# Cross attention on one core: seven late value units, the first loads in single chunks, and the low halves of x ahead of the maxima

## What is computed

```python
# x (32, 512, 640), ctx (32, 77, 1024), 20 heads of 32
q = heads(x @ to_q_w)
k, v = heads(ctx @ to_k_w), heads(ctx @ to_v_w)
p = softmax(einsum('bhqd,bhkd->bhqk', q, k) / sqrt(32))
out = merge(einsum('bhqk,bhkd->bhqd', p, v)) @ to_out_w + to_out_b + x
```

## Time and profile before

| | us |
|---|---|
| time, median of 3 runs | 1733.48 (1733.34 to 1733.49) |
| time of the profiled execution | 1733.08 |
| its span, first to last instruction | 1730.5 |
| TensorE busy | 1706.0 |
| VectorE busy | 1250.5 |
| ScalarE busy | 1082.2 |
| GpSimd busy | 599.3 |

### The profile page before, as it was taken

How to read it: one execution, slowest core, us unless ns; L and a number is a source line. 1 busy time by engine, 2 the same in 40 slices (tenths; PEclk the granted TensorE clock), 3 DMA queues, 4 the chain that set the end, 5 groups by cost and what they waited for, 6 DMA issues and landing times.

```text
span 1730.5 us, 38867 instructions
## 1 busy us (share of the span) xinstructions
PE 1706.0 (99%) x13551; PEld 1365.5 (79%) x13551; DVE 1250.5 (72%) x2525; ACT 1082.2 (63%) x5676; POOL 599.3 (35%) x814
## 2 busy tenths in 40 slices
PE   7999999999999999999999999999999999999998
PEld 7999999767777777777777777777777777777776
DVE  5222123778888888888888888888888888888874
ACT  4322123766767676776767676777767676776762
POOL 0211112433434343343434343333434343333341
PEclk9999999989999999999999999999999999999999
DMA  9544213878989889888979897979797989897965
GB/s 222 169 108 112 68 46 88 217 200 222 239 225 233 237 221 239 223 237 222 238 216 240 218 243 217 246 209 246 211 245 213 245 210 250 211 247 214 244 184 118
DMA packets 311920, 354.43 MB, mean 205 GB/s; under 512 B 40456, under 2 KB 196294, under 8 KB 311726
## 3 DMA queue, kind: packets, MB, share of 16 engines
q1 hardware_dynamic: 241422, 298.38, 64.8%
q10 hardware_dynamic: 66016, 40.97, 10.5%
q0 software_dynamic: 4288, 12.62, 2.1%
HBM read 173.07 MB, written 178.81 MB: 203 GB/s over the span
## 4 chain that ended last, share of the span: by engine, by line
PE 96%; ACT 2%; DVE 0%; DMA 0%; SPq 0%; issue 0%; ACTq 0%
PE p_ring L1099 32%; PE p_ring L1013 31%; PE p_scores L1022 9%; PE p_ring L1056 8%; PE p_bank L439 8%; PE p_bank L458 7%; ACT probs L779 2%; PE p_ring L458 1%; DMA x_raw<-in_L_xattn_to_k_w 0%; PE p_ring L1108 0%; SPq L262 0%; DVE neg_first L847 0%; PE p_scores L1072 0%; ACT x_t L808 0%; ACT o_t L798 0%
## 5 line engine op out<-in xcount | busy, mean ns | idle before, releaser
L742 POOL TENSOR_TENSOR probs<-probs,rsum 128x308 f32<-128x308 f32 x640 | 447.8, 702 | 436.0 <-DVE rsum L862 432.7
L1013 PE MATMUL p_ring<-x_t,wq_split 128*128 128x512 f32 x2400 | 581.5, 394 | 0.0
L1099 PE MATMUL p_ring<-o_t,wo_split 128*128 128x512 f32 x2385 | 568.4, 390 | 0.0
L1013 PEld LDWEIGHTS p_ring<-x_t,wq_split 128*128 128x128 f32 x2400 | 445.2, 188 | 146.9 <-ACT kv_out L790 52.8
L1099 PEld LDWEIGHTS p_ring<-o_t,wo_split 128*128 128x128 f32 x2385 | 446.2, 188 | 107.1 <-ACT kv_out L790 14.3
L779 ACT ACTIVATE probs<-p_scores,neg_first 128x77 f32<-128x77 f32 x1280 | 393.9, 363 | 18.8 <-DVE neg_second L850 18.8
L779 ACT ACTIVATE probs<-p_scores,neg_second 128x77 f32<-128x77 f32 x1280 | 401.5, 444 | 0.0
L779 ACT ACTIVATION_READ_ACCUMULATOR probs<-p_scores,neg_second 128x1 f32 x1280 | 374.9, 326 | 0.0
L870 DVE STREAM_TRANSPOSE turned<-probs 128x384 f32<-128x384 f32 x640 | 353.4, 554 | 26.5 <-POOL probs L742 26.2
L779 ACT ACTIVATION_READ_ACCUMULATOR probs<-p_scores,neg_first 128x1 f32 x1280 | 313.4, 245 | 0.0
L790 ACT ACTIVATE kv_out<-p_ring 128x512 f32<-128x512 f32 x79 | 47.2, 597 | 388.3 <-PE p_ring L1056 388.3
(11 more groups left out here) (48 smaller groups left out, 1186.8 us busy)
## 6 DMA issues: line engine op xcount, KB each, us to landing
p_scratch<-turned SPq DMA_DIRECT2D x158, 768.0 KB, 5.7
probs_t<-p_scratch SPq DMA_DIRECT2D x316, 256.0 KB
x_raw<-in_x ACTq DMA_DIRECT2D x124, 320.0 KB, 7.5
out<-out_blocks SPq DMA_DIRECT2D x124, 320.0 KB, 6.2
probs_t<-p_scratch SPq DMA_DIRECT2D x158, 104.0 KB
ctx_raw<-in_ctx SPq DMA_DIRECT2D x28, 256.0 KB, 7.3
k_sb<-k_scratch SPq DMA_DIRECT2D x32, 192.5 KB, 6.3
v_sb<-v_scratch SPq DMA_DIRECT2D x158, 38.5 KB
```

What stands on the lines that cost most here:

```text
L742: nc.gpsimd.tensor_tensor(heads_of(t), heads_of(t), rsum[:, n % 2, t, :].unsqueeze(2).to_broadcast([P, HG, N_TXT]), ALU.mult).then_inc(pro ...
L1013: last = nc.tensor.matmul(bank_of("Q", n)[:, :], wq_s[:, w, c, g * P:(g + 1) * P], x_t[:, a, c, :], start=c == 0 and i == 0, stop=c == CC ...
L1099: last = nc.tensor.matmul(bank_of("O", n)[:, :], wo_s[:, w, c, k * P:(k + 1) * P], o_t[b % 2][:, o, c, :], start=c == 0 and i == 0, stop=c ...
```

## The change

**Late units.** `LATE_UNITS` gets (8, 1) in front, so there are seven, F0 to F6; each of F0 to F5 now stands for the unit before the one it was. F6 (32 rows, as F5) is a 24-matmul unit in phase 3, between the scores and V. ScalarE's phase 3 is now `S0 S1 F6 K U V S2 ...` instead of `K U V S0 ...`: two tiles of exponentials first. GpSimd's is `F6 W N0 ...`. The last two units share slot 2 of `kv_out` (`out_slot`), since the value copies K use the first two slots; counts of stores per slot follow (`stored_before`), and SyncE waits for F0 to F2 before it issues the first reads of probs. In VECTOR_FIRST the turns Y10 and Y11 go from the end of phase 2 into phase 3, and Q3 of phase 3 goes behind Y13.

**Low halves of x.** For k mod 5 = 4, and so in phase 4 too, VECTOR has `Y14 L12 L13 L14 M W H` where it had `Y14 L13 M L14 W H` with L12 at the end of the phase before. SCALAR has `X14 K U V` where it had `K X14 U V`.

**First loads.** wk's first pair of chunks is loaded as two single chunks; the halves of ctx blocks 0 and 1 are loaded one at a time between wk's pairs, the third pair of chunks between the second half of block 0 and that of block 1. ScalarE, VectorE and TensorE work on the first two blocks in the same way, block 0's slices, the weights, then block 1's, and TensorE runs four units of block 0 for two slices and then four of block 1.

```diff
-                "K X14 U V S0 S1 S2 S3 S4 S5 S6 S7 D3")
+                "X14 K U V S0 S1 S2 S3 S4 S5 S6 S7 D3")
...
-TENSOR_FIRST = orders("S Q2 Q3 F1 F2", "S Q2 F3 F4 Q3", "S V Q2 Q3 F5", "S V Q2 Q3")
+TENSOR_FIRST = orders("S Q2 Q3 F1 F2", "S Q2 F3 F4 Q3", "S V Q2 Q3 F5", "S F6 V Q2 Q3")
...
-    LOADS = ([(wk, k, 2) for k in range(0, KC, 2)] + [(wv, k, 2) for k in range(0, KC, 2)]
+    LOADS = ([(wk, 0, 1), (wk, 1, 1)] + [(wk, k, 2) for k in range(2, KC, 2)] + [(wv, k, 2) for k in range(0, KC, 2)]
...
-    LATE_UNITS = [(BLOCKS - 2, u) for u in (2, 3)] + [(BLOCKS - 1, u) for u in range(VU)]
+    LATE_UNITS = [(BLOCKS - 2, u) for u in (1, 2, 3)] + [(BLOCKS - 1, u) for u in range(VU)]
...
+    def out_slot(n):
+
+        return n % OUTS if n < LATE + 5 else OUTS - 1
+
+    def stored_before(slot, n):
+
+        return DMA * len([i for i in range(n) if out_slot(i) == slot])
+
...
+        def load_first_half(j, half):
+            n0, c0 = j * TB // SQ, half * CK // 2
+            for i in range(I):
+                sp.dma_start(ctx_raw[i * SQ:(i + 1) * SQ, j, :, c0:c0 + CK // 2],
+                             ctx_v[i][:, n0:n0 + TB // SQ, c0:c0 + CK // 2]).then_inc(first_loaded[j][half], DMA)
+
+        load_first_half(0, 0)
         load_weights(range(0, 2))
-        load_first_halves(1)
-        load_weights(range(2, 4))
-        load_weights(range(4, 8))
+        load_first_half(1, 0)
+        load_weights(range(2, 3))
+        load_first_half(0, 1)
+        load_weights(range(3, 4))
+        load_first_half(1, 1)
+        load_weights(range(4, 5))
+        load_weights(range(5, 9))
...
         for u in range(TU):
-            for j in range(2):
-                context_high(j, u)
+            context_high(0, u)
             split_weights(WK[2 * u:2 * u + 2])
+            context_high(1, u)
...
         for u in range(TU):
-            for j in range(2):
-                turn_context(j, u)
-            for j in range(2):
-                context_low(j, u)
+            turn_context(0, u)
+            context_low(0, u)
             split_weights(WK[2 * u:2 * u + 2])
+            turn_context(1, u)
+            context_low(1, u)
...
-        for k in range(KC):
-            pe.wait_ge(w_split, k + 1)
-            for j, m in FIRST[:BANKS]:
-                keys_part(j, m, k)
+        for u in range(TU):
+            for block in range(2):
+                for k in (2 * u, 2 * u + 1):
+                    pe.wait_ge(w_split, k + 1)
+                    for j, m in FIRST[:BANKS]:
+                        if j == block:
+                            keys_part(j, m, k)
...
+                        if k == 1:
+                            sp.wait_ge(project["unit_done"], LATE + 3)
...
-                    project["wait_stored"](act, project["units"] - 1)
+                    project["wait_stored"](act, project["units"] - 2)
```

More of the change, by code:

```diff
@@ L228, in wait_stored @@
         for i in range(OUTS):
-            eng.wait_ge(unit_stored[i], DMA * len(range(i, n, OUTS)))
+            eng.wait_ge(unit_stored[i], stored_before(i, n))
     def sync(sp):
@@ L255, in load_weights @@
                           .then_inc(w_loaded[load], DMA)
-        def load_first_halves(half):
-            c0 = half * CK // 2
-            for j in range(2):
-                n0 = j * TB // SQ
-                for i in range(I):
-                    sp.dma_start(ctx_raw[i * SQ:(i + 1) * SQ, j, :, c0:c0 + CK // 2],
-                                 ctx_v[i][:, n0:n0 + TB // SQ, c0:c0 + CK // 2]).then_inc(first_loaded[j][half], DMA)
-        load_first_halves(0)
-        load_weights(range(0, 2))
-        load_first_halves(1)
-        load_weights(range(2, 4))
-        load_weights(range(4, 8))
+        def load_first_half(j, half):
[4 more added lines that the diff above has]
+        load_first_half(0, 0)
+        load_weights(range(0, 2))
+        load_first_half(1, 0)
[5 more added lines that the diff above has]
+        load_weights(range(5, 9))
         load_block(2)
-        load_weights(range(8, 11))
+        load_weights(range(9, 12))
         load_block(3)
-        load_weights(range(11, 14))
+        load_weights(range(12, 15))
         load_block(4)
@@ L285, in store_key @@
             pool.dma_start(k_scratch[m * P:(m + 1) * P, bass.ds(j * TB, tokens)],
-                           kv_out[:, n % OUTS, 0:tokens]).then_inc(unit_stored[n % OUTS], DMA)
+                           kv_out[:, out_slot(n), 0:tokens]).then_inc(unit_stored[out_slot(n)], DMA)
         def store_value(j, u):
@@ L292, in store_value @@
             pool.dma_start(v_scratch[bass.ds(j * TB + t0, rows), hf * HALF:(hf + 1) * HALF],
-                           kv_out[0:rows, n % OUTS, :]).then_inc(unit_stored[n % OUTS], DMA)
+                           kv_out[0:rows, out_slot(n), :]).then_inc(unit_stored[out_slot(n)], DMA)
         def store_values(j):
@@ L329, in keys_out @@
             if n >= OUTS:
-                act.wait_ge(unit_stored[n % OUTS], DMA * (n // OUTS))
-            nc.scalar.activation(kv_out[:, n % OUTS, 0:tokens], bank_of(n)[:, 0:tokens],
+                act.wait_ge(unit_stored[out_slot(n)], stored_before(out_slot(n), n))
+            nc.scalar.activation(kv_out[:, out_slot(n), 0:tokens], bank_of(n)[:, 0:tokens],
                                  ACT.Copy, scale=SCALE).then_inc(unit_copied, 1)
@@ L337, in value_out @@
             act.wait_ge(unit_done, n + 1)
-            act.wait_ge(unit_stored[n % OUTS], DMA * (n // OUTS))
-            nc.scalar.activation(kv_out[0:rows, n % OUTS, :], source[0:rows, 0:HALF],
+            act.wait_ge(unit_stored[out_slot(n)], stored_before(out_slot(n), n))
+            nc.scalar.activation(kv_out[0:rows, out_slot(n), :], source[0:rows, 0:HALF],
                                  ACT.Copy).then_inc(unit_copied, 1)
```

2 lines of the change are left out of this document (1 added, 1 removed), and 10 rows, old and new, of tables (SCALAR_FIRST, VECTOR, VECTOR_FIRST).

## The result

| | before | changed |
|---|---|---|
| time, median of 13 executions each (us) | 1733.18 (1731.94 to 1734.03) | 1736.43 (1734.07 to 1740.23) |
| ratio to before | | 1.0022, 95% interval 1.0015 to 1.0030 |
| profiled execution: time, span | 1733.08, 1730.5 | 1735.22, 1733.4 |

The forecast was 1734.2 us in a range of 1725 to 1739. The change costs 3.3 us where it was to cost 0.7, and its times spread over 6.2 us where those of before spread over 2.1 (in later sets of 17 executions those of before spread over 2.4 to 4.4 us). Nearly all the profile is as foretold.

What follows compares the result with a forecast made beforehand. The prediction took TensorE's waits and slow stretches to bound the kernel. Start -1.7, seventh late unit -3.8 and low halves +6.2 made +0.7, from 1733.48 to 1734.2 us, range 1725 to 1739.

Steps and rivals of the forecast that it cites:

- What bounds the kernel: Whole kernel: TensorE is busy 1706.0 of 1730.5 us, so a change pays only where TensorE stands or is slow.
- The start: First loads: TensorE starts at 8.65 instead of 12.59, values at 41.1 instead of 42.84; 1.7 us gained.
- what is late next: At the start, the ninth unit waits for the first unit's copy behind a ScalarE weight split, starting at about 35.4.
- that load is limited by bytes that the change does not alter: At the start, wv's chunks 4 and 5 still end loading at 33.35; four extra issues could cost 0.2 us.
- The seventh late unit: Phases 3 and 4: next scores at 16.4, phase 4 ends at 36.7, against 40.5 in all before; 3.8 us gained.
- with no drop of the clock: Phases 3 and 4: the clock stays up, as it fell behind a 3.9 us wait and the longest now is 1.2.
- the second rival: Slower: the clock falls again in phase 3 or 4, costing 4.6 us, to 1738.8; chance 0.12.
- The low halves: Fifth phases: later maxima delay the q copy that frees a bank; 18.28 instead of 17.84, 14 times, 6.2 us lost.
- The first rival: Fifth phases gain as well if the q copy has unseen slack; 2.9 us come back, to 1725.1; chance 0.14.
- The third rival: Late phases gain more than counted, VectorE's queue being 1 to 3 us shorter; 1728 to 1731; chance 0.10.
- The fourth: The start gives nothing, the first unit's copy or store landing later; 1735.9, inside the forecast's own range, no separate chance.
- The sum: Whole kernel: -1.7 - 3.8 + 6.2 = +0.7, from 1733.48 to 1734.2 us.

Runs made afterwards that it cites:

- e6: e3 with the first two copies to kv_out ahead of the split of wv's third pair of chunks on ScalarE; 1724.13 us, ratio 0.9945.
- e10: The changed kernel once more, nothing edited; 1736.58 us over 12 executions, ratio 1.0021 to the kernel before.
- e1: The changed kernel with the old tables for the fifth phases (low halves of x where they were); 1728.08 us, ratio 0.9975.
- e3: The changed kernel with the first q copy of the fifth phases right behind H, in front of the reciprocals; 1724.27 us, ratio 0.9949.
- e4: The kernel before with the new start alone (loads, their split, TensorE's order); 1732.65 us, ratio 0.9997.
- e7: The changed kernel with phase 3's value copies back in front of the exponentials; 1738.73 us, ratio 1.0037.
- e8: e1 with the first q copy of the fifth phases behind H, low halves in their old place; 1727.71 us, ratio 0.9975.
- e2: The kernel before with only the new order of the low halves in the fifth phases; 1740.08 us, ratio 1.0042.
- e5: The kernel before with the seventh late unit alone, old start and old tables for the fifth phases; 1730.75 us, ratio 0.9986.
- e9: e6 with Q3 ahead of Y13 on VectorE in phase 3 and K ahead of X14 on ScalarE in phase 4; 1723.17 us, ratio 0.9941.

## Why the prediction was nearly right

**What bounds the kernel** held: what moved the time were waits of TensorE and its clock.

**The start** (-1.7 foretold, -0.7 in the profile, -0.5 alone by the median): what is late next was named rightly, the copy of the first unit behind the split of wv's third pair, and e6 proves it. The first matmul at 8.22 (8.65 foretold) and the eight units' end at 33.47 (33.9) are close. The step that failed is "that load is limited by bytes that the change does not alter": it took before's 33.35 as fixed, while the split starts at 34.41 in one execution of the changed kernel and 33.24 in another. The copy's time has a scatter of more than 1 us, and in e10's execution the term is 2.1 (first scores at 281.58, 5.58 us earlier, 3.52 of it the unit). Over the profiles with the new start and the copy in its old place (changed, e1, e3, e4, e7, e8, e10) the split starts at 33.24 to 34.41, median 33.90; over those with the old start (before, e2, e5) at 33.35, 33.58 and 32.16. So the prediction read one execution's load as a constant, where it lands 0.5 us later at the median and scatters by about as much each way, in both orders. Why it scatters is open. At the first scores the term is 0.7, 0.9, 1.1, 1.2 and 2.1 us in the five of these profiles in which the clock stays up at the start (changed, e1, e7, e3, e10). The term had a small slip of its own too: it has the ninth unit of before at 37.1, where its own rate gives 12.59 + 24.2 = 36.8 and the trace 37.0, so 35.4 was worth 1.4 to 1.6.

**The seventh late unit** (-3.8): phase 3 at 16.4 (16.37), both phases at 36.7 (36.71), and the waits 0.6, 1.1, 0.55, 1.2, 0.65 came as 0.49, 1.14, 0.29, 1.16, 0.67. The failed step is "with no drop of the clock, since the clock fell behind a wait of 3.9 us and the longest now is 1.2". That holds for the profiled execution and not for all: e5, e6 and e9 have the fall behind the 1.1 us. Its price is 1.6 us in e5 (against e1's phase 4) and 3.5 in e6 (against e3's); for e9's order there is no phase 4 at full clock to compare. So the part is worth 2.4 us by e5's median and not 3.8. This is the second rival, right in its kind, wrong in its condition (the waits joined to one as long as 3.9) and nearly right in its price: 4.6 foretold, and 3.8 between the first and the last row of the table above. Its chance of 0.12 looks too low: 14 of the 25 executions have a mean clock below 0.999.

**The low halves** (+6.2, found +7.2 by the profile, +7.3 alone): maxima at 4.1 (4.04), exponentials 2.17 behind, the copy of q_t as the bank's releaser, 14 waits; e2 shows them, e3 removes them by the copy alone. The first rival (more slack) is refuted by e2's row. The mis-sized term is the wait's price: the stall of 0.65 came as 0.73, and the 0.21 of L14's wait that was to be saved was counted right. L14 in its new place took 0.62 (1.85 / 3) and not 1.23, and GpSimd's subtraction starts at 443.59, 0.3 behind the low parts' end. The Trainium skill (SBUF — State Buffer, Who interferes with whom) says that a VectorE instruction with two SBUF inputs contends with a GpSimd instruction that reads SBUF; the trace agrees, 1.23 us beside the subtraction and 0.62 ahead of it. The maxima, which read PSUM, now run beside the subtraction and keep their 1.43 us. W runs behind it in both kernels, so that it would not be caught no run shows.

**The rest:** phase 1's +0.2 was said to be nothing; it comes with the late units (17.60 in e5, 17.38 in e4), and what in them makes it is open. Phases 0 and 2 kept their lengths (16.6 and 14.8), as foretold, and neither the store slots nor SyncE's new wait shows anywhere. The third rival (late phases shorter than counted) didn't occur. The fourth, that the start gives nothing, is half true.

**The sum** looks better than it is. As a time it is right to a microsecond at full clock: 1734.2 foretold, 1735.2 the median of the executions at 0.999 or more, and the other 1.3 us to the median go with the clock. As a change it was +0.7, and the spans of the two profiles differ by +2.9: the start fell short by 1.0, the fifth phases cost 1.0 more, phase 1 brought 0.2, all in one direction. Some 0.8 of the 2.9 does not reach the times, as the profiled execution of before has 2.58 us outside its span and the changed one 1.8, as most executions of both kernels. That the total still came within a microsecond is partly luck.

## What to carry to other kernels

When instructions move ahead of something in a full queue, look for the copy that frees a bank behind it: here a gain of 2 to 3 us was bought with a stall of over 10, and moving one copy five places forward kept the gain without the stall (1724.3 instead of 1736.4). Where a change is a bundle, cost and run each part alone: two of the three parts here were gains or neutral, and the sum hid it. And if waits of a microsecond stay in a chain that TensorE runs close behind, judge by the median of many executions and their granted clock, since a single profile may show a fall or not show it.

## What the chip showed that was not expected

The clock falls to its lower level behind waits far shorter than the 3.9 us of the earlier trace rows, and not in each execution of the same kernel. Behind a wait of 1.1 us at the head of phase 4 there is none in the profiles of the changed kernel, e1, e3, e8 and e10, and one in those of e5, e6 and e9. e4 has one in phase 2, behind a wait of 0.89 us that stands in the kernel before as well, with no fall there. The scores at its head, and its window:

```profile
321.59 2.02 PE L1035 MATMUL p_scores<-k_sb,q_t 32*128 32x77 f32 x64 [0.89 <-ACT probs L792]
```

```profile
321.58:339.19 17.61, 17.60 (x134) 11.98 (x134) 11.56 (x27) 11.65 (x67) 7.52 (x10) 0.81 0.93 235
```

Phase 2 is 17.61 us there and 14.8 in every other kernel. In e4 and e8 the clock is also at 0.50 for some 3 us from 37.2 and 36.4, behind the wait for the first copy (2.1 and 2.0 us); the 48 matmuls behind it take 7.51 us and not 6.02. In the changed kernel, whose wait was 2.6, it isn't. The Trainium skill (TensorE: Matmul & The Clock Gate, A second HAM failure mode: psum-queue depth-cycling) tells of a kernel whose clock goes up and down because TensorE idles often and briefly between groups of matmuls. These rows agree in that short idle times are enough, but here the clock falls no more than three times in a profiled execution. What decides it in one execution and not in the next no run here shows.
